# Query and key go through a ScalarE copy in SBUF, and GpSimd instead of VectorE splits them, in a four-layer attention and experts kernel

## What is computed

```python
def _attn(xn, Wq, bq, Wk, bk, Wv, bv, Wo, bo, u):
    q = sh(xn @ Wq.T + bq)
    k = sh(xn @ Wk.T + bk)
    v = sh(xn @ Wv.T + bv)
    scores = jnp.einsum('bhqd,bhkd->bhqk', q, k)
    r = _pos_emb(S)
    rel = jnp.einsum('bhqd,ld->bhql', q + u[None, :, None, :], r)
    scores = (scores + _rel_shift(rel, S, S)) * HEAD_DIM ** (-0.5)
    scores = jnp.where(mask[None, None], NEG, scores)
    p = jax.nn.softmax(scores, axis=-1)
    ctx = jnp.einsum('bhqk,bhkd->bhqd', p, v).transpose(0, 2, 1, 3).reshape(B, S, D_MODEL)
    return ctx @ Wo.T + bo
```

## Time and profile before

| | |
|---|---|
| time of three runs, us | 2605.0, 2611.01, 2613.91 |
| median, us | 2611.01 |
| profiled execution, us | 2609.76 |
| its span, us | 2608.0 |
| granted TensorE clock, mean | 0.994 |
| TensorE busy | 2439.1 us, 94% |
| TensorE weight loads busy | 1994.5 us, 76% |
| VectorE busy | 2058.2 us, 79% |
| ScalarE busy | 1853.3 us, 71% |
| GpSimd busy | 1169.0 us, 45% |

### The profile page before, as it was taken

The page is one execution under the profiler, slowest core; times in us unless marked ns, Lnnn a source line. Parts: engine busy times, 40 slices in busy tenths (PEclk is TensorE's granted clock), DMA queues, the critical chain, the costliest instruction groups (busy, mean ns, idle before and its releaser), DMA issues. The chain is left out here.

```text
span 2608.0 us, 81336 instructions
## 1 busy us (share of the span) xinstructions
PE 2439.1 (94%) x31360; PEld 1994.5 (76%) x31360; DVE 2058.2 (79%) x5069; ACT 1853.3 (71%) x2837; POOL 1169.0 (45%) x2072
## 2 busy tenths in 40 slices
PE   0599999999999999999999999999999999598898
PEld 0478888888888888888888888888888887476676
DVE  6488888888888888888888888888888886477774
ACT  1177777777777777877777777777777777454454
POOL 3344444544544444445444444454444443233332
PEclk9999999999999999999999999999999999799999
DMA  4333333333332333333333333333333331100000
GB/s 126 82 85 82 82 88 84 85 85 85 82 86 79 88 82 83 84 84 84 85 82 89 82 83 84 84 85 85 83 82 86 80 83 40 40 25 25 24 21 17
DMA packets 219550, 195.74 MB, mean 75 GB/s; under 512 B 28848, under 2 KB 215344, under 8 KB 219184
## 3 DMA queue, kind: packets, MB, share of 16 engines
q1 hardware_dynamic: 219184, 190.73, 27.1%
HBM read 14.46 MB, written 4.19 MB: 7 GB/s over the span
## 5 line engine op out<-in xcount | busy, mean ns | idle before, releaser
L780 DVE TENSOR_REDUCE rowmax<-bank 128x4 f32<-128x1024 f32 (+1 forms) x768 | 938.5, 1222 | 214.7 <-PE bank L446 214.7
L611 ACT ACTIVATE probs<-bank 128x1024 f32<-128x1024 f32 x768 | 786.6, 1024 | 397.1 <-PE bank L482 382.8
L446 PE MATMUL bank<-kstack,qstack 62*128 62x128 f32 (+1 forms) x4096 | 414.9, 301 | 0.0
L482 PE MATMUL bank<-qstack,kstack 64*128 64x256 f32 (+1 forms) x4096 | 412.1, 300 | 0.0
L650 ACT ACT_TABLE_LOAD x256 | 328.4, 1283 | 4.5
L446 PEld LDWEIGHTS bank<-kstack,qstack 62*128 62x128 f32 x4096 | 292.4, 190 | 3.1
L482 PEld LDWEIGHTS bank<-qstack,kstack 64*128 64x128 f32 x4096 | 290.1, 189 | 3.0
L501 PE MATMUL bank<-probs,v_pad 128*32 128x256 f32 x4096 | 274.7, 386 | 1.5 <-ACT probs L611 1.5
L559 PE MATMUL bank<-w,hidden 128*128 128x128 f32 x2048 | 270.3, 275 | 1.0 <-ACT hidden L657 1.0
L441 PE MATMUL bank<-mask_half,pick_half 64*128 64x128 bf16 (+1 forms) x3072 | 248.4, 240 | 19.6 <-DVE rowmax L780 12.1
L477 PE MATMUL bank<-maskT_half,pick_half 64*128 64x128 bf16 (+1 forms) x3072 | 248.4, 240 | 1.9 <-ACT probs L611 1.9
(11 more groups left out here) (144 smaller groups left out, 5264.7 us busy)
## 6 DMA issues: line engine op xcount, KB each, us to landing
qstack<-base SPq DMA_DIRECT2D x768, 128.0 KB, 2.4
kstack<-base SPq DMA_DIRECT2D x384, 128.0 KB, 2.5
turn_x<-turn_c SPq DMA_DIRECT2D x512, 32.0 KB, 1.8
qstack<-maxrows SPq DMA_DIRECT2D x256, 16.0 KB
xin<-in_x SPq DMA_DIRECT2D x16, 256.0 KB, 2.9
out<-ot SPq DMA_DIRECT2D x16, 256.0 KB, 2.4
w<-in_w SPq DMA_DIRECT2D x4, 256.0 KB, 3.6
w_qkv<-in_w_qkv SPq DMA_DIRECT2D x1, 768.0 KB, 8.1
```

Of the source, the lines that this page charges most:

```text
L446: last = pe.matmul(bank[:, b, i * wide:(i + 1) * wide], qstack[rows, r, p0 + i, t * 128:(t + 1) * 128], kstack[rows, r, p0 + i, 0:wide], s ...
L482: last = pe.matmul(bank[:, 2 + b, i * wide:(i + 1) * wide], kstack[rows, r, p0 + i, kt * 128:(kt + 1) * 128], qstack[rows, r, p0 + i, q0:S ...
L611: act.activation(probs[:, (ROUNDS * n + k) % PR], bank[:, 2:4, :], ACT.Exp, scale=SCALE).then_inc(exp_done, 1)
L780: dve.tensor_reduce(rowmax[:, t, :, p0:p0 + heads], bank[:, 0:2, :].rearrange("p b (h c) -> p b h c", h=heads), AX_X, ALU.max).then_inc(ma ...
```

## The change

ScalarE's `split_first` becomes `qk_out`: it writes query and key with their biases in fp32 to a new tile `qk` in SBUF instead of the first parts to `base`. VectorE's `turn_q` reads the query from `qk` and adds only `u`; `split_rest` goes. GpSimd gets `qk_split` in round 2 behind `v_padded`: a cast of all of `qk` to the first parts, and a subtraction for the second ones. Bank 5 may be overwritten once `qk_out` has run. `qk` is a single buffer, so `qk_out` waits for the previous sequence's `turn_q` and `qk_split`. The sum of `bq` and `u` at the start goes.

```diff
@@ layers_program
-        b_cols = sb("b_cols", [128, LAYERS, 3])
+        b_cols = sb("b_cols", [128, LAYERS, 2])
...
+        qk = sb("qk", [128, 2, S])
...
@@ f1
-                at_least(pe, qk_rest, n)
+                at_least(pe, qk_ready, n)
...
@@ ScalarE
-            def split_first(n):
+            def qk_out(n):
                 act.wait_ge(qkv_done, 2 * n + 1)
-                if n > 0:
-                    act.wait_ge(stack_landed[(n - 1) % RING], 16 * STACK_DMAS * ((n - 1) // RING + 1))
+                at_least(act, qk_rest, n)
+                at_least(act, turn_steps, 2 * n)
                 for src in range(2):
-                    last = act.activation(base[:, 0, src], bank[:, 5, src * S:(src + 1) * S], ACT.Identity,
+                    last = act.activation(qk[:, src], bank[:, 5, src * S:(src + 1) * S], ACT.Identity,
                                           bias=b_cols[:, layer(n), src:src + 1])
-                last.then_inc(qk_first, 1)
+                last.then_inc(qk_ready, 1)
...
@@ VectorE
             def turn_q(n, half):
-                dve.wait_ge(qk_first, n + 1)
+                dve.wait_ge(qk_ready, n + 1)
...
-                dve.scalar_tensor_tensor((turn_s, turn_c)[half][:], bank[:, 5, 0:S],
-                                         b_cols[:, layer(n), 2:3], turn[:, half], ALU.add, ALU.mult
+                dve.scalar_tensor_tensor((turn_s, turn_c)[half][:], qk[:, 0],
+                                         u_cols[:, layer(n), 0:1], turn[:, half], ALU.add, ALU.mult
                                          ).then_inc(turn_steps, 1)
...
-            def split_rest(n):
-                for src in range(2):
-                    last = dve.scalar_tensor_tensor(base[:, 1, src], bank[:, 5, src * S:(src + 1) * S],
-                                                    b_cols[:, layer(n), src:src + 1],
-                                                    base[:, 0, src].bitcast(F32), ALU.add, ALU.subtract)
-                last.then_inc(qk_rest, 1)
...
-            dve.tensor_tensor(b_cols[:, :, 2:3], b_cols[:, :, 2:3], u_cols[:], ALU.add).then_inc(consts_cast, 1)
-            dve.wait_ge(consts_cast, 4)
+            dve.wait_ge(consts_cast, 3)
...
-                        split_rest(s)
...
@@ GpSimd
+            def qk_split(n):
+                pool.wait_ge(qk_ready, n + 1)
+                if n > 0:
+                    pool.wait_ge(stack_landed[(n - 1) % RING], 16 * STACK_DMAS * ((n - 1) // RING + 1))
+                pool.tensor_copy(base[:, 0, 0:2], qk[:]).then_inc(qk_first, 1)
+                pool.wait_ge(qk_first, n + 1)
+                pool.tensor_tensor(base[:, 1, 0:2], qk[:], base[:, 0, 0:2].bitcast(F32), ALU.subtract
+                                   ).then_inc(qk_rest, 1)
...
                     if k == 2 and live(s - 2):
                         v_padded(s - 2)
+                    if k == 2 and live(s):
+                        qk_split(s)
                     if k == 3 and live(s - 5):
                         xn2_split(s - 5)
```

More of the change, by code:

```diff
@@ L262, in layers_program @@
         rot_ready = sem("rot_ready")
+        qk_ready = sem("qk_ready")
         qk_first = sem("qk_first")
@@ L565, in _ @@
             pe.wait_ge(squares_landed, 48)
-            pe.wait_ge(consts_cast, 4)
+            pe.wait_ge(consts_cast, 3)
             pe.wait_ge(prefilled, 2)
@@ L664, in _ @@
             act.wait_ge(consts_landed, 16 * CONST_DMAS)
-            act.wait_ge(consts_cast, 4)
+            act.wait_ge(consts_cast, 3)
             act.wait_ge(prefilled, 2)
@@ L674, in _ @@
                     if k == 0 and live(s):
-                        split_first(s)
+                        qk_out(s)
                     if k == 1 and live(s - 4):
@@ L868, in _ @@
             pool.wait_ge(consts_landed, 16 * CONST_DMAS)
-            pool.wait_ge(consts_cast, 4)
+            pool.wait_ge(consts_cast, 3)
             def power(ve, mv, rstd, mv_sem, ve_sem, rstd_sem, n):
@@ L1413 @@
                                 axis=1).transpose(0, 2, 1),
-        "b_cols": np.stack([bq[:, feature], i("L0_attn_bk")[:, feature], bq[:, feature]], axis=1).reshape(LAYERS * 3, D).T,
+        "b_cols": np.stack([bq[:, feature], i("L0_attn_bk")[:, feature]], axis=1).reshape(LAYERS * 2, D).T,
         "u_cols": u[:, feature].T,
```

## The result

The changed kernel takes 2623.7 us (median of 6 runs, 2622.52 to 2626.84), the kernel before 2610.65 us in the same comparison: 1.0051 times as long, with a 95% interval of 1.0038 to 1.0064. The profiled execution took 2626.84 us, 3 us more than the median, with a span of 2625.0 us.

A forecast was written before the change was run, and what follows sets the result against it. TensorE's pace, with short waits for VectorE's reductions, was taken as the bound. A loss of 18.3 us in ordinary slots, 3 at layer boundaries and 2 in the fill made 23, so 2633 us, range 2604 to 2645.

The forecast's parts named there:

- What bounds the kernel: Attention layers: TensorE's own pace, busy 99.69 of 100 us, plus three short waits for VectorE's reductions per slot.
- The relief: `split_rest` off VectorE: reduction 2 starts earlier and round 3 is no longer held, a gain of 0.05 us a slot.
- ScalarE, SyncE, and `turn_q` from SBUF: Ordinary slots: activations and new waits, later content DMAs, and `turn_q` reading SBUF were each taken to cost nothing.
- The collision: Round 2: both `apply_1` instructions on VectorE wait for GpSimd's new subtraction and next cast; round 4 loads 0.15 us later.
- the rule of overlap less 0.14: A GpSimd instruction meeting a VectorE one in SBUF is delayed by their overlap less 0.14 us; 0.07 for L905.
- The size: Net loss of 0.15 us a slot, round 3's gain included; over about 122 slots 18.3 us.
- the lag behind it: The held `apply_1` instruction on VectorE ends 0.09 us after GpSimd's subtraction, the middle between 0.04 and 0.155.
- a margin of 0.05: Round 4 loads 0.11 us after reduction 3 ends where 0.06 suffices, leaving 0.05 us before a delay counts.
- rival 1: Only the first `apply_1` instruction is held, the second precedes GpSimd's cast: 12 us slower, 2622 us; chance 0.17.
- Layer boundaries: At three boundaries `split_w1` holds the second `turn_q` and a later subtraction holds `apply_1`: near 1.0 us each, 3 us.
- The fill: While the pipeline fills, cast and `turn_q` start at the same signal: two to four slots at up to 1 us, 2 us.
- the one on waits: ScalarE's new waits, `qk_rest` and `turn_steps` of the sequence before, are met some ten microseconds ahead and cost nothing.

The follow-up runs named there:

- experiment 2: The kernel before with `split_rest` computing only one of 256 columns, nothing added on GpSimd: 2601.1 us, 0.9974.
- experiment 3: The changed kernel with `turn_q` reading the query from bank 5 in PSUM again: 2618.83 us, 1.0044 times the kernel before.
- experiment 4: The changed kernel with `qk_split` moved on GpSimd behind `xn2_split` and `add_row` of round 3: 2603.77 us, 0.9989 times the kernel before.
- experiment 7: The changed kernel with `apply_1` moved on VectorE to the front of `turn_q` in round 1: 2604.45 us, 0.9985 times the kernel before.
- experiment 6: The kernel before with `split_rest` cut to one column and three GpSimd powers of 128x2 numbers behind `v_padded`: one run of 2595.8 us.
- experiment 5: The changed kernel with `qk_split` behind `add_row` of round 3 and `turn_q` from bank 5 in PSUM: 2600.26 us, 0.9971 times the kernel before.
- experiment 8: The kernel before with a GpSimd cast and subtraction of 128x256 on spare tiles behind `v_padded`: one run of 2606.3 us.
- experiment 1: The kernel before with a GpSimd cast and subtraction of 128x512 on tiles nobody else reads, behind `v_padded`: 2624.12 us, 1.0067.

## Why the prediction was right, point by point

Forecast were 2633 us, 23 more than before, in a range from 2604 to 2645; measured were 2623.7, 13 more. The mechanism was the one forecast, and the size was 1.8 times too large: the loss of a slot was taken too high, and the start-up had the wrong sign.

*What bounds the kernel.* Right: TensorE's pace plus the few places where it waits for a reduction. The relief is worth 0.049 us between the reductions around the held round, and 0.063 over the whole slot (experiment 2), where 0.05 was forecast.

*ScalarE, SyncE, and `turn_q` from SBUF.* Each was costed at nothing in ordinary slots; experiments 3, 4 and 7 agree to within 0.02 us a slot.

*The collision.* Right in its place, its two instructions and its consequence. It rested on a single instruction that had held GpSimd, L905 at 1868.50, and on the rule of overlap less 0.14; that VectorE would be the one held was inferred. In the changed kernel all ordinary slots show the reverse, VectorE held. By the two pages of the Trainium skill that the prediction named (SBUF — State Buffer, "two separate sides", and VectorE: DVE Perf Modes, perf-mode tier table), an fp32 `tensor_scalar` in SBUF is exposed to GpSimd; the trace agrees (998 ns instead of 340). The Trainium skill (SBUF — State Buffer, "two separate sides") has the lock last for the whole of an instruction. The casts and subtractions here agree, but experiment 6 does not: powers of 0.7 us on 128x2 numbers held nothing.

*The size.* 0.15 us a slot was forecast, 0.106 came. The table of distances shows where it went: the subtraction ended 0.02 us sooner, the lag behind it was 0.08 each time instead of 0.09, and the sum of rounded durations up to the load was 0.01 to 0.02 too long. Together 0.05, small in each term and a third of the result, because the result is what is left of 0.2 us after a margin of 0.05. The 12 us of rival 1 came close to the measured total by luck, not by its mechanism: it had the second instruction slip in before the cast, and it takes 418 ns in nearly every slot.

*Layer boundaries.* 1.0 us each was forecast; 17.67 less 16.63 is 1.04. The path is the forecast one, the second `turn_q` held to the end of the weights' subtraction and the pair by a later `qk_split`.

*The fill.* This term had the wrong sign. I costed the start at +2 us, for a cast and `turn_q` on the same signal. The collision is there: in the third sequence the first `turn_q` takes 1.34 us, and the first four slots are 1.2 us longer in sum, where with `turn_q` from PSUM (experiment 3) they are 0.2 longer. But the first reduction of all starts at 91.00 us instead of 93.66. The step that failed is the one on waits: I looked for what the new waits add and not for what the one removed, on `stack_landed`, had held. Before, ScalarE in the second sequence waited for the content transfers:

```profile
84.98 0.84 ACT L633 ACTIVATE base<-bank,b_cols 128x256 fp32r<-128x256 f32 x2 [5.46 <-DMA kstack<-base]
```

After, it writes `qk` as soon as the products are there, and only GpSimd waits for the transfers:

```profile
82.39 0.84 ACT L634 ACTIVATE qk<-bank,b_cols 128x256 f32<-128x256 f32 x2 [3.00 <-PE bank L110]
```

*The sum.* From span to span, +17.0 us: -2.7 up to the first reduction, +17.5 from the first reduction to the last, +2.2 behind it, in code that the change does not touch and whose length varies between 401 and 407 us over all traces of this study. The 17.5 are 123 slots at 0.106 (13.0), what three of them, the boundaries, take beyond that (3 x 1.04 = 3.1), the first four slots (1.2) and three slots that were longer once for no reason that I found (0.5), less 0.3 for the last two, in which nothing is split any more. Forecast were 18.3 + 3 + 2 = 23. Without the part behind the layers it is 14.9, and the medians differ by 13.1.

## What to carry to other kernels

Before work moves to GpSimd, write down for VectorE which instructions have two inputs in SBUF or are copies and tensor-scalar operations from SBUF to SBUF, and see whether one of them, with TensorE waiting behind it, falls into the new work's time; instructions with an input in PSUM ran beside it freely here. If one does, try another place in either engine's list: here it cost nothing and turned the loss into the gain, with GpSimd's work moved (experiment 4) and with VectorE's (experiment 7). A held instruction shows in its mean duration (521 instead of 340 ns), not as idle time, so VectorE's busy share hides it.

## What the runs showed of the hardware that was not expected

- VectorE held by GpSimd ends 0.08 us after GpSimd's instruction for 128 columns of TENSOR_SCALAR, behind a subtraction and behind a cast alike. For 128x256 of SCALAR_TENSOR_TENSOR with both inputs in SBUF (`turn_q` at the boundaries) it is 0.28 us.
- GpSimd's powers on 128x2 numbers, 0.7 us each, do not hold VectorE, where a subtraction of 128x512 of 1.27 us does to its end. Whether it is the reading or the writing that holds, from what size on, and whether the kind of operation matters, was not tried.
- SCALAR_TENSOR_TENSOR of 128x256 with one input in PSUM takes 475 ns, with both in SBUF 477.
- Kernels in which the same waits are left differ by a few hundredths of a microsecond a slot: 16.493 (experiment 4), 16.469 (5), 16.464 (2), 16.433 (6); from end to end that is 7 us over the whole kernel. In the kernel before, slots of 16.51 and 16.53 alternate in runs of several. What sets this is open. It does not lie where the collision does. From reduction 1 to reduction 4 of a slot the medians are 6.495 to 6.504 us in experiments 2, 4, 5, 6 and 7, against 6.544 before, 6.541 in experiment 8, and 6.637 to 6.651 in the changed kernel and experiments 1 and 3, so gain and loss stand clear of the spread there. The rest of the slot takes 9.97 to 9.99 us in all but experiment 6 (9.93).
- The 0.02 us of experiment 3 in ordinary slots come back when experiment 4 becomes 5 by the same edit (16.493 to 16.469). They lie for the most part in that rest of the slot, not in the duration of `turn_q`. They may belong to its source or to the spread; no run here tells which.
